# Weighted sum of gathered rows: scaling moved from ScalarE to VectorE, with four partial sums

## What is computed

```python
final_scores, pk_idx = jax.lax.top_k(score, FINAL_TOPK)              # FINAL_TOPK = 16
final_indices = jnp.take_along_axis(index, pk_idx, axis=-1)
final_scores = jax.nn.softmax(final_scores, axis=-1)
...
# keys and values: sum over the 16 of final_scores * table[final_indices]
```

## Time and profile before

| | us |
|---|---|
| median of 3 runs | 8664.17 |
| lowest, highest run | 8647.6, 8669.62 |
| span of the profiled execution | 12469.6 |
| VectorE busy in the profiled execution | 5016.0 (40%) |
| ScalarE busy | 3311.9 (27%) |
| TensorE matmuls busy | 6502.1 (52%) |
| GpSimd busy | 5950.0 (48%) |

### The profile page before, as it was taken

One profiled execution on the slowest core, in us unless ns is written; L12 is line 12 of the kernel. 1 busy time (PEld: TensorE's weight loads), 2 busy tenths in 40 slices (PEclk: granted clock), 3 DMA queues, 4 the chain that ended last, 5 costly groups with the idle time before them and its releaser, 6 DMA issues.

```text
span 12469.6 us, 153471 instructions
## 1 busy us (share of the span) xinstructions
PE 6502.1 (52%) x51536; PEld 4676.4 (38%) x51536; DVE 5016.0 (40%) x16213; ACT 3311.9 (27%) x9871; POOL 5950.0 (48%) x6157
## 2 busy tenths in 40 slices
PE   7845364555645566464654645555565555424203
PEld 6633243442534434343343433444344433213102
DVE  2253524435253443525345253452524435352612
ACT  2212222223222232222322222222322223222222
POOL 0024545445454554545455454454545445565573
PEclk7755555556555565555555555555555555555555
DMA  1011111111111111111111111111111111111110
GB/s 29 12 28 39 44 38 43 37 38 40 35 42 39 41 39 37 45 35 41 36 40 42 35 41 39 39 41 36 38 40 42 38 36 41 39 42 39 41 49 25
DMA packets 251313, 474.14 MB, mean 38 GB/s; under 512 B 130470, under 2 KB 130974, under 8 KB 250143
## 3 DMA queue, kind: packets, MB, share of 16 engines
q0 software_dynamic: 196608, 403.05, 12.2%
q1 hardware_dynamic: 53856, 60.52, 1.7%
HBM read 461.04 MB, written 2.10 MB: 37 GB/s over the span
## 4 chain that ended last, share of the span: by engine, by line
issue 30%; PE 29%; DVE 17%; another core or an unknown queue 16%; DVEq 5%; ACT 3%; DMA 0%; SPq 0%; ACTq 0%; POOL 0%; POOLq 0%
PE MM L417 3%; DVE KV L849 3%; PE PB L1107 3%; PE PB L1080 2%; ACT GATH L842 2%; PE PB L1145 2%; DVEq L823 2%; PE PB L1104 2%; PE PB L1121 2%; PE PB L1135 1%; PE MM L371 1%; DVE I L786 1%; DVE PF L824 1%; PE MM L432 1%
## 5 line engine op out<-in xcount | busy, mean ns | idle before, releaser
L624 POOL DMA_INDIRECT GATH<-in_table,IDX x6144 | 5946.4, 968 | 6393.3 <-DVE KV L849 3878.1
L842 ACT ACTIVATE GATH<-GATH,WT 128x128 f32<-128x128 f32 x6144 | 1902.5, 392 | 198.0 <-issue 197.1
L849 DVE TENSOR_REDUCE KV<-GATH 128x128 f32<-128x2048 f32 x384 | 1390.7, 3622 | 679.4 <-ACT GATH L842 407.6
L417 PE MATMUL MM<-SPEC,SW 32*32 32x8 f32 x25600 | 613.6, 196 | 1688.7 <-issue 1646.1
L417 PEld LDWEIGHTS MM<-SPEC,SW 32*32 32x32 f32 x25600 | 519.8, 147 | 1800.0 <-issue 1792.4
L485 ACT ACTIVATE U<-MM 128x320 f32<-128x320 f32 (+1 forms) x416 | 219.5, 528 | 1853.3 <-remote 879.6
L526 DVE COPY TURN<-TP 80x512 f32<-80x512 f32 (+1 forms) x512 | 347.2, 685 | 890.1 <-remote 440.0
L485 ACT ACTIVATE SPEC<-MM 128x160 f32<-128x160 f32 x320 | 96.1, 301 | 2238.0 <-PE MM L417 1423.5
L371 PE MATMUL MM<-F,TURN 128*128 128x80 f32 x2048 | 422.9, 375 | 442.0 <-DVE TURN L526 350.6
L371 PEld LDWEIGHTS MM<-F,TURN 128*128 128x128 f32 x2048 | 391.8, 284 | 506.0 <-issue 266.4
L456 PEld LDWEIGHTS MM<-G,TURN 80*128 80x128 f32 x2048 | 344.9, 241 | 522.7 <-issue 243.8
(11 more groups left out here) (201 smaller groups left out, 11175.6 us busy)
## 6 DMA issues: line engine op xcount, KB each, us to landing
GATH<-in_table,IDX POOLq DMA_INDIRECT x6144
SW<-in_sw SPq DMA_DIRECT2D x160, 320.0 KB
CONV<-in_cwb SPq DMA_DIRECT2D x128, 4.0 KB
CONV<-in_cwb SPq DMA_DIRECT2D x128, 0.1 KB
U<-in_xT SPq DMA_DIRECT2D x16, 96.0 KB
out<-OUTB SPq DMA_DIRECT2D x16, 96.0 KB
W1E<-in_w SPq DMA_DIRECT2D x1, 520.0 KB
W2E<-in_w SPq DMA_DIRECT2D x1, 512.0 KB
```

Of the source, the lines that this page charges most:

```text
L417: m = e.matmul(pv[r, :, k, :], SW[r, c % 2, k, :], Sv[r, :, c * MODES + k, :], start=True, stop=True)
L624: e.indirect_dma_start(GATH[:, r, k, :], None, table, bass.IndirectOffsetOnAxis(IDX[:, u // H, u % H, k:k + 1], 0)).then_inc(gath[r], 16)
L842: m = e.activation(GATH[:, r, k, :], GATH[:, r, k, :], ACT.Copy, scale=WT[:, u // H, u % H, k:k + 1])
L849: e.tensor_reduce(KV[:, u // H, u % H, :], GATH[:, u % RING, :, :].rearrange("p k d -> p d k"), AX.X, ALU.add).then_inc(S["gather_free"], 1)
```

## The change

ScalarE's `a_consume` goes, and with it the semaphore `multiplied`. `v_consume` does the whole unit on VectorE: it waits for the gather itself; four products by tensor_scalar (tile times weight column) start four partial sums in a new tile `PART`; twelve fused multiply-adds (scalar_tensor_tensor) follow in three groups of four; two additions, 128x256 and 128x128, join the four sums. There is a drain ahead of the unit, one behind each group and one between the additions. The marks are u + 0.3, then u + 0.42, u + 0.54, u + 0.66, so that other VectorE work can come between the groups. The buffer is released by the last addition. The wait for `kept_idx` goes, since VectorE writes `WT` itself. The loop over `CANDIDATES` now uses the names r0 and r1, so the waits behind it in `v_top` are made with the pair's number.

```diff
-        GATH = sb("GATH", [128, RING, TOPK, 2 * D]); KV = sb("KV", [128, NT3, H, 2 * D])
+        GATH = sb("GATH", [128, RING, TOPK, 2 * D]); KV = sb("KV", [128, NT3, H, 2 * D]); PART = sb("PART", [128, 4, 2 * D])
...
-                    for i, n, j, m in CANDIDATES:
+                    for r0, n, r1, m in CANDIDATES:
...
-        def a_consume(e, i, u):
-
-            yield u
+        def v_consume(e, i, u):
+
+            yield u + 0.3
             r = u % RING
+            e.drain()
             e.wait_ge(gath[r], (i * (NT3 * H // RING) + u // RING + 1) * 16 * TOPK)
-            e.wait_ge(*event("kept_idx", i, u // H + 1))
-            for k in range(TOPK):
-                if k in (4, 8, 12): yield u + 0.03 * k
-                m = e.activation(GATH[:, r, k, :], GATH[:, r, k, :], ACT.Copy, scale=WT[:, u // H, u % H, k:k + 1])
-            m.then_inc(S["multiplied"], 1)
-
-        def v_consume(e, i, u):
-
-            yield u + 0.6
-            e.wait_ge(*event("multiplied", i, u + 1))
-            e.tensor_reduce(KV[:, u // H, u % H, :], GATH[:, u % RING, :, :].rearrange("p k d -> p d k"), AX.X, ALU.add).then_inc(S["gather_free"], 1)
+            for n in range(0, TOPK, 4):
+                if n: yield u + 0.3 + 0.03 * n
+                for k in range(n, n + 4):
+                    w = WT[:, u // H, u % H, k:k + 1]
+                    if n: e.scalar_tensor_tensor(PART[:, k % 4, :], GATH[:, r, k, :], w, PART[:, k % 4, :], ALU.mult, ALU.add)
+                    else: e.tensor_scalar(PART[:, k, :], GATH[:, r, k, :], w, None, ALU.mult)
+                e.drain()
+            e.tensor_tensor(PART[:, 0:2, :], PART[:, 0:2, :], PART[:, 2:4, :], ALU.add); e.drain()
+            e.tensor_tensor(KV[:, u // H, u % H, :], PART[:, 0, :], PART[:, 1, :], ALU.add).then_inc(S["gather_free"], 1)
```

More of the change, by code:

```diff
@@ L256, in early_fusion @@
                "rden": 2, "shift_top": NT3, "exp_top": NT3, "kept_idx": NT3, "kept_x": 1,
-               "gather_free": NT3 * H, "weighted": 1, "maxed5": 12, "scaled5": 6, "out_sb": 1, "stored": 16, "multiplied": NT3 * H}
+               "gather_free": NT3 * H, "weighted": 1, "maxed5": 12, "scaled5": 6, "out_sb": 1, "stored": 16}
         S = {n: sem(n) for n in PER}
@@ L793, in v_top @@
                     at = 0
-                    for i, n, j, m in CANDIDATES:
-                        e.tensor_tensor(dst[:, :, at:at + n * m], src[:, 0, :, i:i + n].to_broadcast([128, H, m]) if n == 1 else src[:, 0, :, i:i + n],
-                                        src[:, 1, :, j:j + m].to_broadcast([128, H, n]) if m == 1 and n > 1 else src[:, 1, :, j:j + m], ALU.add)
+                    for r0, n, r1, m in CANDIDATES:
+                        e.tensor_tensor(dst[:, :, at:at + n * m], src[:, 0, :, r0:r0 + n].to_broadcast([128, H, m]) if n == 1 else src[:, 0, :, r0:r0 + n],
+                                        src[:, 1, :, r1:r1 + m].to_broadcast([128, H, n]) if m == 1 and n > 1 else src[:, 1, :, r1:r1 + m], ALU.add)
                         at += n * m
@@ L1314, in SCALAR @@
                     "tokens": lambda: a_tokens(e, g), "rnn": lambda: a_rnn(e, j), "moe": lambda: a_moe(e, j), "att": lambda: a_att(e, j),
-                    "pk": lambda: a_pk(e, j), "top": lambda: a_top(e, j), "back": lambda: a_back(e, k),
-                    "rows": units(a_consume, e, i)}
+                    "pk": lambda: a_pk(e, j), "top": lambda: a_top(e, j), "back": lambda: a_back(e, k)}
         def VECTOR(e, k, i, j, g, l):
@@ L1357, in before @@
             def before(e):
-                credits(e, ["exped", "exp_top", "multiplied"])
+                credits(e, ["exped", "exp_top"])
                 e.sem_inc(mm_out, CREDIT); e.sem_inc(mm_full, CREDIT)
```

## The result

The changed kernel takes 8788.44 us (8774.59 to 8801.16), the kernel before 8656.11 us on the same chip: a ratio of 1.0158, 95% interval 1.0140 to 1.0176. It is 132 us slower, where the prediction had 51 us faster. The time lies inside the wide range of the prediction (8420 to 8850), outside the forecast's own (8490 to 8670), and on the other side of the kernel before.

A forecast was written before the change was run, and what follows sets the result against it. The prediction took TensorE to bound each pair's first half and VectorE the second, gathers close below; -125 + 69 + 54 - 49 = -51 on 8664 gave 8613 us, own range 8490 to 8670, wide range 8420 to 8850.

The forecast's parts named there:

- The issue time: Chain time in which an engine waits for nothing recorded, 30% of 12469.6 us: claimed to be made by the recording, absent from runs.
- 271 + 223 = 494 us: First and second half of a pair without issue time: TensorE claimed to bound the first, VectorE the second.
- 3% of room: GpSimd's gathers, 480 us a pair against 494: claimed not to bind yet, but to be the floor of any gain.
- -125 for ScalarE's pieces: ScalarE's scalings taken off the chain: half of their 249 us claimed as gain, -125 us.
- The 249 us: ScalarE's scalings on the chain, 2% of 12469.6 us; as full relief a rival at 0.16, 8435 us, with the waits 8280.
- +69 and +54 for VectorE's units: Second halves: units at 4.5 us, +0.9 each; +69 us for those on the chain, +54 for half the covered ones.
- -49 for shorter blocks: First halves: VectorE's longest block ahead of a copy for TensorE falls from 3.62 to 1.75 us, -49 us over 26 units.
- the 5.6 of the other bound: VectorE's unit at 5.6 us, +2.0, if a weight per partition forbids overlap of its instructions.
- The gathers' rival: GpSimd's gathers slowed beside two-input multiply-adds, 0.1 to 0.3 us each, +190 us at worst, 8850; decides above 20.6 us a unit; chance 0.06.
- VectorE decides the second half: Rival: all 13 units of 15 second halves lie on the path, 8780 to 8994 us, typically 8800; chance 0.25.
- The new waits: VectorE's waits for the gather and for Exp: buffers claimed to cover the gather, Exp 33 us early, 0 us.
- tensor_scalar and GpSimd: VectorE's products beside gathers: the skill says two-port tensor_scalar shuts GpSimd out; the prediction found no row before showing it.

## Why the prediction was wrong, point by point

- **The issue time, the step that failed first.** The prediction took the 30% of "issue" as made by the recording. The recording of the lower level shows a span of 8656.8 us beside runs of 8655 us, so it makes nothing; the pauses are in timed runs too where a chip has them. The trace was of another regime than the times, and a page whose span is 44% above the median says so: its shares aren't to be rescaled. That 70% of the span came within 1% of the median proved nothing about which engine is the bound.
- **What bounds the kernel.** The pair was put at 271 + 223 = 494 us by taking the issue time out, the gathers at 480, "3% of room". They were the bound already: 488.5 us a pair from the second to the fifteenth, of which 480 are 384 gathers of 0.945 with 0.305 us between them, and 8 are hold-ups. The numbers for that stood in the rows: 5946.4 and 6143 x 0.30 are 7790, and with the 665 us ahead of the first gather and the 126 us behind the last one in that trace 8581 of the 8664 us. What was missing was to put this sum against the median before anything else.
- **-125 for ScalarE's pieces.** Measured: -3 us, interval -18 to +1 (the kernel without scaling). The 249 us were 2% of the chain of the upper level; at the lower level ScalarE waits 1722.5 us for the gathers, and all its work is 1% of the chain. The term is absent, not eaten up.
- **+69 and +54 for VectorE's units, -49 for shorter blocks.** They priced a path that isn't the bound. Their unit was too cheap besides: a step of 195 ns for the products (taken 0.14 us) and of 262 ns for the multiply-adds (taken 0.20), so a unit is 5.4 us at least, not 4.5. Neither did a weight for each partition forbid overlap (the 5.6 of the other bound): four multiply-adds take 1.13 us in the timeline above, 0.345 each alone. VectorE's busy time rose by 536 us, not 350. By "VectorE: DVE Perf Modes" of the Trainium skill, "The DRAIN you can't avoid", each would wait for the one before; the same section adds that a next operation that isn't held starts earlier, which the prediction left out, and the timeline shows that second case (its advice on the number of operations stands in "Rules for kernel authors" of that page). The 5.6 us came nearer than my 4.5 all the same, by chance.
- **The gathers' rival, at 0.06.** It was the mechanism at this level. Its size was right in kind (0.1 to 0.3 us each expected, 84 ns on the mean measured, for 2.5 gathers of a unit instead of 3.6), its threshold wrong: "above 20.6 us a unit" came from the 494 us. With the gathers back to back it decides from the first nanosecond; a unit of gathers went from 20.36 to 20.74 us.
- **VectorE decides the second half, at 0.25.** Typically 8800, measured 8788: the number is near by luck. In the changed kernel's trace GpSimd waits only some 12 us for VectorE behind the first pair, so VectorE is not what decides; at the change's own load it is a bound 26 us below, and it is what answers if the gathers are relieved.
- **The new waits.** Exp: no wait of VectorE for it is in the changed kernel's trace, as predicted. The wait for the gathers (479.6 us ahead of L845) is idle time on an engine that is ahead, as ScalarE's 1722.5 was.
- **tensor_scalar and GpSimd.** The Trainium skill's section named above has the two-port forms of tensor_scalar shut GpSimd out. In the kernel with products only, a gather beside one of the 6144 products is 21 ns longer (1175 of them), against 84 beside multiply-adds: small here. No run shows whether these products ran in a two-port form.

## What to carry to other kernels

Before any chain is read, add up each engine that does one thing at a time from start to end, durations and the pauses between them, and put the sum against the timed median; here it came within 1%, and that engine was the bound whatever it seemed to wait for in a profile of another regime. A kernel bound by GpSimd's gathers is moved by what VectorE runs beside them: in these runs instructions with one SBUF input (reductions, products) cost the gathers little or nothing, and long ones with two inputs cost less in pieces of some 0.35 us, so long as VectorE had room. Eight pieces were worse than four, so the size has to be tried. Work taken from an engine that waits for the bound gains nothing, and where it lands decides the sign.

## What the runs showed of the hardware

- An indirect DMA of 128 rows of 512 B took 0.944 to 0.947 us of GpSimd in the median of each trace, with 0.305 us before the next; from start to start it was 1.25 us in the median, and never under 1.24 in the two kernels' traces at the lower level.
- It was lengthened by VectorE instructions with two SBUF operands that ran at its start: by 84 ns on the mean beside a 128-column multiply-add in the changed kernel (13 ns where the multiply-adds stood ahead of the reduction, at the upper level), by 379 ns on the mean beside L818 (0.82 to 0.99 us long), up to 2.31 us in all where L561, L818 and L821 followed each other. Beside the reduction L849 not at all (1085 gathers); beside the short reductions that filled up VectorE between products by 20 ns (246 gathers).
- scalar_tensor_tensor and tensor_scalar with a weight for each partition, 128 columns, one behind the other: a start each 262 and 195 ns, 345 and 281 ns long.
- The same kernels took 1.44 to 1.46 times as long on two chips as on the others, with pauses of TensorE's and VectorE's issue while GpSimd gathers. There the change gave 0.9982, and 384 gathers less gave 463 us. No cause is shown.
